# The last combination of the experts' results, shared out from one engine to three

## The reference, cut to what matters

```python
x = x + _L0_attn_a_ref(_layernorm(x), ...)
x = x + _L0_ffn_ref(_layernorm(x), ...)
x = x + _L0_attn_b_ref(_layernorm(x), ...)
x = x + _L0_ffn_ref(_layernorm(x), ...)     # its last step is the one changed

def _L0_ffn_ref(x, gate_w, gate_b, w1, b1, w2, b2):
    ...                                      # 2 of 24 experts per token, y: their results
    out = jnp.einsum('bse,besd->bsd', combine, y)   # two rows per token, each by its gate
    return out + x
```

## Time and profile before

| | us |
|---|---|
| median of 3 runs | 788.13 (787.86 to 789.38) |
| span of the profiled execution | 791.8 |
| DVE busy in it | 529.6 (67%) |
| ACT busy in it | 405.3 (51%) |
| POOL busy in it | 414.8 (52%) |
| PE busy in it | 642.2 (81%) |

### The profile page before, as it was taken

How to read it: one execution, slowest core, us unless ns; L and a number is a source line. 1 busy time by engine, 2 the same in 40 slices (tenths; PEclk the granted TensorE clock), 3 DMA queues, 4 the chain that set the end, 5 groups by cost and what they waited for, 6 DMA issues and landing times.

```text
span 791.8 us, 17837 instructions
## 1 busy us (share of the span) xinstructions
PE 642.2 (81%) x4583; PEld 434.2 (55%) x4583; DVE 529.6 (67%) x1518; ACT 405.3 (51%) x880; POOL 414.8 (52%) x488
## 2 busy tenths in 40 slices
PE   4974888888865599999287799999888648999890
PEld 2311333324653499999143355555456517999890
DVE  6779999996565266555378889899645633665444
ACT  2645777772321165665075567677644303566550
POOL 5203999985667255454277534444444672545450
PEclk9965999999995799999699599999999867999995
DMA  7979999922011122221618311211002112222215
GB/s 205 321 254 256 251 247 249 249 58 80 8 34 47 53 81 70 72 72 41 185 36 287 128 51 49 59 49 35 4 0 98 34 53 58 78 71 67 67 42 166
DMA packets 88312, 84.43 MB, mean 107 GB/s; under 512 B 12897, under 2 KB 77401, under 8 KB 87977
## 3 DMA queue, kind: packets, MB, share of 16 engines
q1 hardware_dynamic: 82600, 71.89, 33.9%
q0 software_dynamic: 5632, 11.58, 4.5%
HBM read 37.98 MB, written 45.46 MB: 105 GB/s over the span
## 4 chain that ended last, share of the span: by engine, by line
PE 33%; DVE 7%; issue 5%; DMA 2%; SPq 2%; ACT 2%; POOL 1%; ACTq 0%; DVEq 0%; POOLq 0%
PE bank L643 7%; PE bank L652 6%; PE bank L2017 5%; PE bank L1948 3%; PE bank L1951 2%; DVE t_peak L1768 2%; PE bank L2127 2%; PE bank L1993 2%; PE bank L2118 1%; DVE X L249 1%; PE bank L636 1%; SPq L1427 1%; DMA work<-results 1%; PE bank L2044 1%; DVE t_tabs L1848 0%
## 5 line engine op out<-in xcount | busy, mean ns | idle before, releaser
L806 POOL TENSOR_TENSOR UN<-work 128x512 f32<-128x512 f32 x64 | 81.7, 1289 | 55.4 <-DVE work L1034 54.7
L1768 DVE TENSOR_REDUCE t_peak<-bank 128x1 f32<-128x512 f32 (+2 forms) x192 | 104.0, 592 | 9.5 <-PE bank L1951 7.4
L445 ACT ACTIVATE t_v_tiles<-bank,t_e_b1all 128x128 f32<-128x128 f32 x224 | 64.0, 368 | 63.5 <-PE bank L643 58.8
L445 ACT ACTIVATE m_dx_tiles<-bank,m_e_b1all 128x128 f32<-128x128 f32 x224 | 64.0, 369 | 60.0 <-PE bank L643 57.8
L410 POOL DMA_INDIRECT results<-t_A,t_e_to_row x56 | 53.8, 961 | 67.1 <-DVE t_A L559 33.0
L410 POOL DMA_INDIRECT results<-m_XC,m_e_to_row x56 | 53.8, 961 | 63.7 <-issue 33.9
L1181 PE MATMUL bank<-UN,ident 128*128 128x512 f32 x128 | 71.0, 637 | 14.2 <-POOL UN L806 13.6
L1034 DVE TENSOR_TENSOR_SCAN work<-bank,work 128x512 f32<-128x512 f32 x64 | 76.6, 1216 | 8.3 <-POOL UN L806 7.0
L549 DVE COPY UN<-w1all 128x512 f32 x112 | 48.2, 430 | 40.5 <-PE bank L643 28.4
L652 PE MATMUL bank<-w2all,t_v_tiles 128*128 x448 | 60.6, 279 | 2.7 <-ACT t_v_tiles L445 2.0
L643 PE MATMUL bank<-t_A,UN 128*128 128x128 f32 x448 | 61.0, 280 | 0.0
(11 more groups left out here) (323 smaller groups left out, 1441.8 us busy)
## 6 DMA issues: line engine op xcount, KB each, us to landing
xrows<-m_nothing SPq DMA_DIRECT2D x25, 1032.0 KB, 17.9
w1all<-in_e_w SPq DMA_DIRECT2D x6, 1024.0 KB, 12.2
work<-results SPq DMA_DIRECT2D x16, 256.0 KB, 4.5
m_dx_tiles<-xrows SPq DMA_DIRECT2D x56, 64.5 KB
t_v_tiles<-xrows SPq DMA_DIRECT2D x56, 64.5 KB
t_tabs<-stacks SPq DMA_DIRECT2D x32, 96.0 KB, 2.2
work<-stacks SPq DMA_DIRECT2D x32, 96.0 KB, 2.1
m_tabs<-in_e_b SPq DMA_DIRECT2D x1, 1536.0 KB
```

What stands on the lines that cost most here:

```text
L445: ins = act.activation(e.hid[:, mp, f * P:f * P + P], core.tiles(2 + mp)[:, f, :], ACT.Gelu, bias=row(e.b1all, x)[:, f:f + 1])
L806: g.tensor_tensor(hc[:, k % 4, :], h[:, k % 2, :], c_sb[:, k % 2, :], ALU.mult).then_inc(hc_ready, 1)
L1768: v.tensor_reduce(peak[p][:, a, ss[0]:ss[-1] + 1, qt], bank[:, f, 0:len(ss) * w].rearrange("p (j n) -> p j n", n=w), AX_X, ALU.max).then_i ...
```

## The change

The tiles of each batch are split. VectorE keeps tiles 0, 1, 2 of batches 0 and 2 and tiles 0, 1 of batches 1 and 3, ten in all, and combines them as before. For each of the other six tiles ScalarE multiplies `back[0]` by its gate in place and then `back[1]` (an activation Identity with a scale per partition), and GpSimd adds each of them to X. GpSimd waits for each scaled tile, and before a tile's second addition for its own first one. The store of a batch now waits for VectorE's tiles and for GpSimd's. The first mixture's combination keeps all tiles on VectorE.

```diff
+ON_DVE = ((0, 1, 2), (0, 1), (0, 1, 2), (0, 1))
+ON_POOL = tuple(tuple(t for t in range(4) if t not in x) for x in ON_DVE)
...
-def combine(v, core, added, b, layer):
+def combine(v, core, added, b, layer, tiles=range(TT)):
 
-    tiles = range(b * TT, b * TT + TT)
+    tiles = [b * TT + t for t in tiles]
     v.wait_ge(core.back_in[b], 16 * TOPK * layer)
+    before = b * TT if layer == 1 else sum(len(ON_DVE[x]) for x in range(b))
     for k in range(TOPK):
         if k:
-            v.wait_ge(added[0], b * TT + TT)
+            v.wait_ge(added[0], before + len(tiles))
         for i in tiles:
             v.scalar_tensor_tensor(out=core.X[:, i, :], in0=core.back[k][:, i, :], scalar=core.gate[:, k, i:i + 1],
                                    in1=core.X[:, i, :], op0=ALU.mult, op1=ALU.add).then_inc(added[k], 1)
...
+        if layer == 2:
+            self.scaled, self.pool_added = sem("scaled"), sem("pool_added")
...
             for b in range(NB):
-                sp.wait_ge(e.added[1], b * TT + TT)
+                sp.wait_ge(e.added[1], sum(len(ON_DVE[x]) for x in range(b + 1)))
+                sp.wait_ge(e.pool_added, TOPK * sum(len(ON_POOL[x]) for x in range(b + 1)))
                 sp.dma_start(core.out[b].rearrange("(t p) d -> p t d", p=P), core.X[:, b * TT:b * TT + TT, :])\
                     .then_inc(e.stored, 16)
...
                                  e.ysb[:, j % 4, :], None).then_inc(core.y_out[j % 4], 16)
+        if e.layer == 2:
+            g.wait_ge(e.skip_added, NT)
+            n = 0
+            for b in range(NB):
+                for i in (b * TT + t for t in ON_POOL[b]):
+                    for k in range(TOPK):
+                        n += 1
+                        g.wait_ge(e.scaled, n)
+                        if k:
+                            g.wait_ge(e.pool_added, n - 1)
+                        g.tensor_tensor(core.X[:, i, :], core.X[:, i, :], core.back[k][:, i, :], ALU.add).then_inc(e.pool_added, 1)
...
         e.steps(act, step)
+        if e.layer == 2:
+            act.wait_ge(e.gate_step, 3)
+            for b in range(NB):
+                act.wait_ge(core.back_in[b], 16 * TOPK * e.layer)
+                for i in (b * TT + t for t in ON_POOL[b]):
+                    for k in range(TOPK):
+                        x = core.back[k][:, i, :]
+                        act.activation(x, x, ACT.Identity, scale=core.gate[:, k, i:i + 1]).then_inc(e.scaled, 1)
...
         if layer == 2:
             for b in range(NB):
-                combine(v, core, e.added, b, layer)
+                combine(v, core, e.added, b, layer, ON_DVE[b])
```

## The result

The changed kernel took 789.93 us in the median of seven runs (788.84 to 792.17), the kernel before 787.86 us on the same chip (seven runs, 785.60 to 789.38). The ratio is 1.005, with a 95% interval of 1.0031 to 1.0069: +3.9 us, from 2.4 to 5.4. The interval does not reach 1: the change makes the kernel slower. The difference of the two medians is only 2.1 us, so the size is known less well than the sign.

The account below looks back on a forecast made before the run. VectorE's combination, with the last loads close behind, was taken to bound the end. GpSimd's additions to 788.8, its DRAIN 6.6 and 0.2 more gave 795.6 against 791.8: +3.8, so 791.9 us, range 787.4 to 793.5.

Parts of the forecast that it names:

- What comes off VectorE: Last combination: twelve of 32 VectorE instructions go, 3.4 us; VectorE ends 2.3 us earlier, as loads take the rest.
- as fast as alone: Evidence against exclusion: VectorE's eight L249 instructions beside GpSimd work took 0.276 us each, as fast as without it.
- GpSimd's additions: Last combination: twelve at 0.53 us, +0.1 on six beside VectorE; they end at 788.8, range 788.2 to 789.8.
- ScalarE's scaling: Last combination: twelve 128x128 scalings, 0.48 us alone, 0.39 from one to the next; ahead of GpSimd throughout.
- The DRAIN: Last block's end: GpSimd's DRAIN starts after its last addition, costs 6.6 us more and ends at 795.4.
- the two readings: Last block's DRAIN: first, a routine costing the same whenever it starts; second, something finishes by itself, leaving it nearly free.
- The middle of 6.0 and 7.3 us: DRAIN time after GpSimd's last instruction, taken as 6.6 us: 7.3 counted from the indirect DMA's end, 6.0 from its landing.
- one routine: The first reading: GpSimd runs a routine at a DRAIN with indirect DMAs behind it, same cost whenever it starts.
- The sum: Span end: DRAIN ends at 795.4, plus 0.2 makes 795.6 against 791.8, +3.8 us; 791.9 us from the median.
- The free DRAIN: Rival at the last block's end: DRAIN nearly free, end set by additions and store, -0.3 us, 787.8 us; chance 0.34.
- Exclusion for whole instructions: Rival: VectorE and GpSimd run one behind another to 790.8; 789.8 us (free DRAIN, chance 0.03) or 793.9 (paid, 0.07).

Follow-up runs that it names:

- experiment 6: The changed kernel with each of GpSimd's twelve additions made a memset of the scaled tile, six tiles left uncombined; ran once, 790.98 us.
- experiment 1: The kernel before with one wait added: GpSimd waits for VectorE's last combination instruction before its DRAIN; ratio 1.0064 to the kernel before.

## Why the prediction was right

**What comes off VectorE: wrong in size.** The forecast had VectorE ending at 13.0 us on the scale of the last DMA; it was 14.5. Alone it is 13.3: 0.3 us over the forecast, which had batch 2 start at 10.0 us, in the middle between its neighbours, where it started after 10.3 (experiment 6, and the changed kernel). The other 1.2 us are GpSimd's reading beside it. The step that failed is "as fast as alone", read off L249's eight in 2.28 us: the GpSimd instructions beside those eight worked on 128x4 values only, and L222 among them ran for 1.24 us, so being beside VectorE for long is not enough; what part of a full-sized addition does it, no run here takes apart. The nearer row for VectorE would have been a GpSimd addition of a tile beside a two-input VectorE instruction. This error cost the forecast nothing, and that was luck of a kind: VectorE ends before GpSimd in both accounts, and only GpSimd's end sets when the DRAIN starts.

**GpSimd's additions: the end right, by two errors that cancel.** Their end came at 14.9 against 15.0. The forecast put +0.1 us on six additions, as VectorE was to be done by then. Measured, ten additions took 5.75 us instead of 5.12, so +0.06 each, and on all ten, since VectorE was at work almost to their end. A single one took 0.45 to 0.60 us beside VectorE, 0.45 alone. ScalarE's scaling took 0.39 us instead of 0.48 and hid as forecast.

**The DRAIN: right, and it decided.** Of the two readings the first holds; experiment 1 shows it with no work moved. The middle of 6.0 and 7.3 us was the wrong choice within it: it is 7.3 from the end of the last GpSimd instruction, as the reading from the end of the indirect DMA had it. What I called one routine is 0.082 us times 88. That both blocks had the same 88 stood in the earlier trace rows; it could not be told from a fixed price there, and the forecast did not need to.

**The sum.** +4.5 us in the profiled tail against +3.8: +0.7 from the DRAIN, nothing from the additions. Timed, +3.9 by the ratio (2.4 to 5.4), +2.1 by the two medians. The forecast of 791.9 us took the first median, 788.13, and the difference whole; the median of the changed kernel is 789.93. That the ratio's +3.9 lies so near to +3.8 is chance: the runs of one kernel scatter by some 4 us, more than this difference, and the tail, which is the sharper measure, says 0.7 us more than forecast.

**The rivals.** The free DRAIN fell (experiment 1). Exclusion for whole instructions fell too: it had GpSimd end at 17.0 us on this scale (790.8 - 773.8), and it was 14.9. But the two engines do hold each other up, and VectorE lost 1.2 to 1.3 us by it.

## What to carry to other kernels

Before work is put on an engine that was idle at the end, look at what its queue holds after that work: here a DRAIN of 8.4 us that lay hidden and became the end of the kernel when it was made to start late. Look for such a sequencer instruction in the block's own lines, since the chain of waits shows only what ended last. And if a wait or a DRAIN is taken out, ask which later instruction will pay for it.

## What the runs showed of the hardware

GpSimd's DRAIN takes 0.082 to 0.084 us for each indirect DMA of 128 rows since its last DRAIN: 7.25 us for 88 when it starts late, 8.44 when it is recorded from before the last one, 5.814 for 56 in that same way, 2.67 for 32, 0.041 for none. It does not end before the last one has landed: 2.44 us behind a single one that landed after 2.22, 3.70 where that took 3.48. A VectorE instruction with two SBUF inputs of 128x128 grows from 0.346 us to a median of 0.536 beside GpSimd additions of two SBUF tiles, and not at all beside GpSimd memsets.
